# Band loads of a windowed attention kernel: the six key and query terms on every second partition

## What is computed

```
q = _lin(Q, wq_w[2], wq_b[2]).reshape(Bx, Nq, h, d)
k = _lin(patches, wk_w[2], wk_b[2]).reshape(Bx, Nq, WIN * WIN, h, d)
v = _lin(patches, wv_w[2], wv_b[2]).reshape(Bx, Nq, WIN * WIN, h, d)
attn = jax.nn.softmax(jnp.einsum('bnhd,bnwhd->bnhw', q, k) * scale, axis=-1)
y_win = jnp.einsum('bnhw,bnwhd->bnhd', attn, v).reshape(Bx, Nq, C)
```

## Time and profile before

| what | value |
|---|---|
| median of three runs | 883.44 us (882.57 to 892.22) |
| profiled execution | 886.04 us, its span 884.3 us |
| mean granted TensorE clock | 0.898 |
| PE busy | 739.2 us (84%) |
| VectorE busy | 636.1 us (72%) |
| ScalarE busy | 354.8 us (40%) |
| GpSimd busy | 175.5 us (20%) |
| DMA queue q10 (ScalarE's) | 22.24 MB, 11.9% of 16 engines |
| DMA queue q1 (SyncE's) | 43.08 MB, 20.9% of 16 engines |

### The profile page before, as it was taken

The page is one execution under the profiler, slowest core; times in us unless marked ns, Lnnn a source line. Parts: engine busy times, 40 slices in busy tenths (PEclk is TensorE's granted clock), DMA queues, the critical chain, the costliest instruction groups (busy, mean ns, idle before and its releaser), DMA issues.

```text
span 884.3 us, 14113 instructions
## 1 busy us (share of the span) xinstructions
PE 739.2 (84%) x5053; PEld 384.9 (44%) x5053; DVE 636.1 (72%) x1330; ACT 354.8 (40%) x609; POOL 175.5 (20%) x239
## 2 busy tenths in 40 slices
PE   4949867878699999968788888888888999999993
PEld 2526432433244444435444444444443445455551
DVE  6976445565599999967665666666666898999960
ACT  2160324443433344414444444334453332447656
POOL 1110113233254444416000000000041044700000
PEclk9965788988779999988988989888899999999997
DMA  5000155555499000005766666656310000000000
GB/s 213 0 1 0 26 134 145 137 127 153 121 203 167 4 1 1 1 14 154 139 127 118 129 126 140 128 118 135 57 24 2 0 0 1 1 0 37 36 37 36
DMA packets 52518, 66.21 MB, mean 75 GB/s; under 512 B 10590, under 2 KB 48226, under 8 KB 50594
## 3 DMA queue, kind: packets, MB, share of 16 engines
q1 hardware_dynamic: 49282, 43.08, 20.9%
q10 hardware_dynamic: 3168, 22.24, 11.9%
HBM read 43.03 MB, written 21.57 MB: 73 GB/s over the span
## 4 chain that ended last, share of the span: by engine, by line
PE 37%; DVE 20%; DMA 8%; issue 5%; ACT 4%; SPq 0%; POOL 0%; DVEq 0%; ACTq 0%
PE banks L853 12%; DMA Q<-nT 5%; PE banks L793 5%; PE banks L777 5%; PE banks L755 4%; DVE mx L1224 4%; DVE sm L1237 3%; PE banks L808 3%; DMA FP<-nT 3%; DVE AC L1056 2%; DVE wn L1291 2%; DVE X L1319 2%; DVE sm L1239 2%; PE banks L739 1%; DVE SEB L1227 1%
## 5 line engine op out<-in xcount | busy, mean ns | idle before, releaser
L955 ACT ACTIVATE P<-banks 126x480 f32<-126x480 f32 (+2 forms) x196 | 100.7, 520 | 164.5 <-PE banks L777 153.7
L1291 DVE TENSOR_REDUCE wn<-banks 128x4 f32<-128x728 f32 x112 | 101.7, 911 | 67.4 <-PE banks L755 66.3
L853 PE MATMUL banks<-FP,PTB 128*128 128x392 f32 x384 | 129.2, 493 | 1.4 <-DVE c L1322 1.2
L1056 DVE SCALAR_TENSOR_TENSOR AC<-XT,vec,AC 128x1540 f32<-128x1540 f32 (+5 forms) x48 | 115.1, 2401 | 1.1
L853 PEld LDWEIGHTS banks<-FP,PTB 128*128 128x128 f32 x384 | 72.8, 190 | 55.8 <-DVE c L1322 1.9
L793 PE MATMUL banks<-P,Vw 126*17 126x120 f32 (+2 forms) x1568 | 79.4, 279 | 0.0
L501 POOL TENSOR_TENSOR SEB<-SEB,rg 112x392 f32<-112x392 f32 x112 | 58.3, 542 | 86.1 <-DVE rg L1244 86.1
L1153 DVE TENSOR_TENSOR pr<-pf,pk 128x434 f32<-128x434 f32 (+1 forms) x42 | 31.8, 758 | 56.7 <-ACT pk L910 56.1
L485 POOL TENSOR_TENSOR pk<-pr,pk 128x434 bf16<-128x434 f32 (+1 forms) x42 | 42.7, 1018 | 138.8 <-DVE pk L1164 138.8
L777 PE MATMUL banks<-Q,K 128*128 128x120 bf16 (+2 forms) x504 | 49.9, 228 | 20.8 <-DMA Q<-nT 20.1
L934 ACT ACTIVATE SEB<-SEB 112x424 f32<-112x424 f32 x56 | 31.2, 557 | 85.7 <-DVE SEB L1227 83.8
(11 more groups left out here) (227 smaller groups left out, 1269.8 us busy)
## 6 DMA issues: line engine op xcount, KB each, us to landing
k_parts<-pk SPq DMA_DIRECT2D x84, 108.5 KB, 2.8
Vw<-v_rows SPq DMA_DIRECT2D x84, 66.9 KB
q_parts<-pk SPq DMA_DIRECT2D x42, 112.0 KB, 2.7
K<-k_parts ACTq DMA_DIRECT2D x7, 651.0 KB, 6.1
v_rows<-vst SPq DMA_DIRECT2D x14, 263.5 KB
X<-in_x SPq DMA_DIRECT2D x2, 1568.0 KB, 8.3
out_y<-zs SPq DMA_DIRECT2D x8, 392.0 KB, 2.4
K<-k_parts ACTq DMA_DIRECT2D x7, 434.0 KB, 4.9
```

The costliest lines, as they stand in the source:

```text
L853: last = mm(bank(2 + place_in_unit, C, ZPIX), WT[:, dy, part, C * grp:C * (grp + 1)], D[:, part, QROWS * q + dy:QROWS * (q + 1) + dy, :].r ...
L955: a(P[q % 4][0:BKEYS[b], 0:4 * BQ[b]], PS[0:BKEYS[b], 4 + q % 2, 0:4 * BQ[b]], ACT.Exp).then_inc(sem("w_exp"), 1)
L1056: return ve.scalar_tensor_tensor(out=o, in0=src(ro + dy, rn, co + dx, cn), scalar=v(wcol + t), in1=o, op0=ALU.mult, op1=ALU.add)
L1291: ve.tensor_reduce(dst, src, AX.X, ALU.max, negate=True).then_inc(sem("w_slot_read"), 1)
```

## The change

`TRUNS` gets new first partitions, and the two destinations in `load_band` step by two. The 48-row load goes to partitions 0, 2, ... 94, the 32-row load to 33, 35, ... 95, the 16-row load to 1, 3, ... 31. Sources, sizes, queues and order of all instructions are the same on each engine, and so are the 32 rows from partition 96 on.

```diff
-TRUNS = ((0, 48, 3), (1, 16, 2), (2, 0, 1))
+TRUNS = ((0, 0, 3), (1, 33, 2), (2, 1, 1))
...
             qpart, r0, n = TRUNS[part]
             src = k_dram[0:n, :, img, t].rearrange("t d h n -> d t (h n)")
-            queue.dma_start(K[j % BUFS][r0:r0 + DH * n, 0:HEADS * KBAND], src).then_inc(done, 16)
+            queue.dma_start(K[j % BUFS][r0:r0 + 2 * DH * n - 1:2, 0:HEADS * KBAND], src).then_inc(done, 16)
             src = q_dram[qpart, :, img, t].rearrange("d h n -> d (h n)")
-            queue.dma_start(QB[j % BUFS][r0:r0 + DH * n, 0:HEADS * BAND], bc(src.unsqueeze(1), [DH, n, HEADS * BAND])).then_inc(done, 16)
+            queue.dma_start(QB[j % BUFS][r0:r0 + 2 * DH * n - 1:2, 0:HEADS * BAND], bc(src.unsqueeze(1), [DH, n, HEADS * BAND])).then_inc(done, 16)
```

## The result

The changed kernel has a median of 847.19 us (four runs, 842.57 to 847.83) against 883.91 us (four runs) of the kernel before on the same chip: the ratio is 0.9554, its 95% interval 0.9487 to 0.9622. The span of the profiled execution is 845.0 us instead of 884.3.

The account below looks back on a forecast made before the run. It took TensorE's waits for the shift DMA behind band loads, and the clock falling after them, as the cost. Waits 18.2 + clock 18 - 2 given back = 34 us off the profiled 886.04 gives 852, median 849; range 836 to 874.

Parts of the forecast that it names:

- The shift stands behind the 32-row load: Step 8: TensorE waits for a small shift DMA; a load issued just ahead costs it some 2.9 us.
- The 32-row load gets faster because it reaches more ports: Load ahead of the shift: two rows to each of 16 ports, 26 to 27 GB/s; gain taken as 1.4 us.
- The wait: TensorE's wait for the shift in step 8 falls from 2.64 to about 0.95 us; ten jobs give 17.0 us.
- The wait of 1.23 us ahead of the ten jobs: One more TensorE wait for the shift, expected to go as a whole, within the 18.2 us for waits.
- The clock: Window-stage jobs: the clock no longer falls behind the shorter wait; 18 us taken, bounds 0 and 18.7.
- Given back: Window stage: shorter jobs pack DMA work more densely and other waits surface; 2 us lost, an estimate.
- The 48-row load: Now over 95 partitions; could go from 16.0 towards 26.3 GB/s or stay; no change taken.
- The 16-row load: Issued in step 7: rate from 7.6 to about 13.7 GB/s; the reciprocals behind it gain, and need to.
- A: Rival: the waits shrink but the clock still falls, only 16 us go, 867 us; chance 0.17.
- B: Rival: the shift lands within 2.9 us, no wait is left, 46 us go, 837 us; chance 0.12.
- C: Rival: no change, the shift is held by something independent of partitions, or by one row at most; chance 0.10.
- D: Rival: the 48-row load slows, sums come late and VectorE stands in step 7; fully 913 us; chance 0.06.

Follow-up runs that it names:

- e1: Kernel before, dense partitions kept, with the 32-row load issued in step 5 of a job instead of step 3, behind the shift: 927.74 us, ratio 1.0496.
- e4: Same DMAs and order as e3 on other partitions, the 32-row load on 0, 2, ... 62: 885.06 us, ratio 1.0012 to the kernel before.
- e3: Changed kernel with its 48-row load cut in two, 32-row and 16-row loads left in place; control for e4: 858.11 us, ratio 0.9714 to the kernel before.
- e5: e3 with the 16-row load dense again on 0 to 15 and a third of the 48-row load on 16 to 31: 855.41 us, ratio 0.9662.
- e2: Kernel before with 12 more matmuls, results overwritten, in step 8 of jobs 1 to 11 ahead of the wait for the shift: 871.28 us, ratio 0.9878.
- e9: Changed kernel with the 16-row load in step 3, ahead of the shift, and the 32-row load in step 7: 844.18 us, ratio 0.9517 to the kernel before.
- e6: Kernel before, dense partitions, with the 16-row load in step 3, ahead of the shift, and the 32-row load in step 7: 861.23 us, ratio 0.9728.

## Why the prediction was right, step by step

It said 849 us (836 to 874); 847.19 was measured. The mechanism was the one forecast. The medians differ by 36.7 us and the profiled executions by 39.3, where the sum had 34. The terms were these:

- *The shift stands behind the 32-row load*: shown. e1 takes the load away from in front of it and the waits go; e4 puts the load back on eight ports and they return.
- *The 32-row load gets faster because it reaches more ports*: shown by e3 against e4. Its rate went from 13.7 to 20.1 GB/s, not to the 26.3 that was taken, so that by the rates its 42.1 KB per engine take 2.1 us instead of 3.1. Its landings fell by 1.2 and 1.8 us, around the 1.4 us of the term: that the term came out is in part luck.
- *The wait*: 0.50 us a job was left (5.0 us in the ten jobs) instead of 0.95. In these jobs the waits fell from 26.4 to 5.0 us, by 21.4 where the sum had 17.0. This term was undersized. Of the 0.3 us in it that were to come from the 16-row load e5 shows 0.1 at most. The wait shrank by 2.1 us a job, and the load by 1.0 (rates) to 1.8 (query rows' landing); what the difference is stays open.
- *The wait of 1.23 us ahead of the ten jobs*: it went as forecast, but its time did not come back, since the first "Y" starts no earlier. TensorE waits there longer for VectorE, 1.75 us at 406.54 and 1.79 us at 415.75 where it was 1.41 and 1.21, and the mean clock from 410 to 420 us is 0.67 (0.83 before).
- *The clock*: forecast 18 us. It is at 1.00 in all ten jobs. Of the 39.4 us that they gained, 39.4 - 21.4 = 18.0 are not waits for the shift, and e2 found 1.8 us a job with the loads untouched. But the reason that the prediction gave for it, a wait shorter than the 1.23 us that left the clock up, was too weak. Seven us ahead of that row the same trace has a wait of 1.21 us, for VectorE, behind which the clock fell:

```profile
415.31 0.27 PE L763 MATMUL banks<-identb,wnb 128*8 128x128 bf16 x2 [1.21 <-DVE wn L1291]
```
```profile
415.31:420.62 5.31, 5.31 (x73) 3.21 (x73) 3.81 (x13) 2.28 (x4) 0.77 (x1) 0.68 0.90 205
```

- *Given back*: 2 us were put down, nothing came. The jobs last 16.33 us on average, where 17.0 were asked for and 16.2 was the floor.
- *The 48-row load*: no gain was taken, and none came (6.1 to 5.9 us, rate 16.0 to 15.2). By the rule of the Trainium skill ("SBUF — State Buffer", Door 1) its fullest ports are as full as before, and the trace agrees.
- *The 16-row load*: its rate rose past the forecast 13.7 to 16.7 GB/s, and it lands in 3.6 us instead of 5.5. That the reciprocals "need to" gain was too strong: e5 keeps it dense, the reciprocals come late by 6.7 us in all, and the median shows no loss.

Of the rivals, A (the clock falls all the same) was priced for waits of 1.2 to 1.9 us; they are 0.5, and no wait of TensorE's matmuls in the ten jobs is above 0.85. B (everything goes, 837) was too low: e9, in which under 1 us of waits for the shift is left, still measures 844. C (nothing moves) is out. With the turns between queues (the Trainium skill, "DMA: Bandwidth & Descriptors", Queues, rings and completion order) the prediction went too far. The Trainium skill says there that an engine drains a whole packet, typically 9 to 17 descriptors, before it turns to another queue. That this is one row of a load is the prediction's reading and not the skill's. What the runs show is that the shift waits for more than one row: 1.17 us a job behind one key row and one query row per engine (e6), 2.64 behind two of each. They do not tell whether its data or only the signal of its completion waited, and so they do not speak against the skill. D (a slower 48-row load) did not happen.

## What to carry to other kernels

Look at which DMA an engine waits for, and then at what was issued just ahead of it: the small transfer paid for the large one, though nobody waited for the large one. Before moving a load out of one transfer's way, look at what it is moved in front of; here moving a load by two steps took away waits of 2.6 us and brought others of 5. And a wait on TensorE has a second price in the clock behind it, which a job-by-job table of the granted clock shows at once; if the wait can't go, some matmuls in it may pay for themselves.

## What was not expected of the hardware

- Twelve useless matmuls of 336 columns in a wait of 2.6 us took 1.2% off the kernel by the medians (e2): the clock stayed at 2.4 GHz, and in the profiled execution 1.8 us a job came back.
- The length of one wait did not say whether the clock would fall. In the kernel before it fell behind the ten waits of 1.97 us and more, and also behind one of 1.21 us, but stayed up behind 1.23; in e3 and e5 it fell behind 1.54, 1.87 and 1.62 us, in e6 it stayed up behind 1.64, and in e4 behind 1.80 and 2.14:

```profile
464.10:469.00 4.90, 4.88 (x91) 2.95 (x92) 2.96 (x6) 2.66 (x5) 0.00 (x0) 1.00 0.28 58
```

- Sixteen rows on 16 adjacent partitions, one per DMA engine, landed 0.8 to 1.0 us sooner than 32 rows on 32 (e6), although both are dense. As the 16-row load of the kernel before, in step 7 with other traffic, the same rows took 5.5 us.
- Moving one pair of DMA issues by two steps cost 5% (e1), more than the whole change gained.
